# Recommender tower on one core: gathered fields first, the last tile in two parts

## The chip, the core and the metric

One core of a Trainium2 chip. The metric is the device time of one execution in microseconds. Before the change it is 455.31 us, the median of three runs (454.63 to 456.35). All times in the profile count from the start of the profiled execution's span.

## The reference

For each of 2048 samples, 50 embedding rows of 16 numbers are looked up, one per field. All 1225 dot products of two different rows go, with 16 dense numbers, through an MLP of 512, 256 and 1 units:

```python
e = jnp.stack([tbl_0[ids[:, 0]], ..., tbl_49[ids[:, 49]]], axis=1)
gram = jnp.einsum('bid,bjd->bij', e, e)[:, I_IDX, J_IDX]     # pairs i < j
...                                    # relu(cat(gram, dense) @ W_top1 + b_top1), and so on
```

29 tables have 1000 or 1250 rows ("small"), two of the 12500-row tables are called medium here, and 19 ("rest") have 12500 or 125000 rows.

## The kernel before

A tile is 128 samples; there are 16 (0 to 15; `LAST` is 15), four to a chunk; `FINAL` = 12 is the first tile of the last chunk.

**Fields.** The 19 rest fields of a tile are gathered by GpSimd, one indirect DMA per field (`gathers`, L448), through a ring of four tiles. Small and medium fields are looked up a chunk ahead as one-hot products: VectorE builds the one-hots (`compare`), TensorE multiplies (`look_up`), ScalarE copies out (`copy_lookups`), VectorE picks by the id's low bits (`pick`), and ScalarE moves the results into `split` (`move`, L1056 and L1065: 16 activations per chunk, all in the first slot of the chunk that uses them). VectorE reads a tile's gathered rows as high and low halves (`split_rows`, L576 to L589; in a chunk's first tile it waits for all moves) and turns them (`turn`, L604: `turned`, `turned2`).

**Dots.** TensorE makes all 50 x 50 dot products of a tile in small matmuls, four row groups of 32 (`dots`, L820, four groups per tile; in the last chunk `half_dots`, L841, eight halves). The results are evacuated from PSUM to `gram`: up to tile 11 by ScalarE alone (`copy_dots`, L1010), in the last chunk by ScalarE and VectorE (`copy_half`, L1018 and L644).

**Packing.** DMAs copy pieces of `gram` into `z`, 127 partitions by 11 columns, so that the first layer is 11 matmuls deep: 9 pieces for each of two sides, 18 issues on SP (`pack`, L383). For tile 15 SP, ScalarE and GpSimd issue six each. Pieces have 44, 33, 22 or 11 rows of 2816 B and five times 5 rows of 1280 B.

**MLP.** ScalarE makes the high half of z (`split_products`, L1077), VectorE the low half (L552); the first layer is 33 matmuls (`first_layer`, L881): 22 high, 11 low. Relu, transposes, layer 2 (L938), and the score on VectorE (L704, L706) follow.

**Order.** Each engine and each DMA queue runs its instructions in the order written. In slots 0 to 12, TensorE's slot T holds the dots of tile T-1, the MLP of T-3 and lookups, in eight groups; ScalarE evacuates in groups 1, 3, 5 and 7 and splits the products of T-2 in group 4. GpSimd is held only by semaphores of tile T-3 (`pace`) and T-4. The last chunk's order is written out by hand, differently on each engine. Tile 15's first nine gathered rows are read and turned together with the looked-up fields (`last_rows(0)`, L620 to L636), the last ten when they land (`last_rows(1)`); its dots wait for both:

```python
                if h == 0:
                    pe.wait_ge(turned_ready, 2 * T + (2 if T < LAST else 4))
```

Among its dots stand 16 of tile 14's 22 high matmuls (L902). Tile 15's own first layer goes in two parts by columns (L854, L858).

Of the kernel before, what the change touches and what calls it, by code (L numbers as in the profile page):

```python
# [10 lines left out]
ALU = mybir.AluOpType  # L11
# [33 lines left out]
FIELD = SMALL[:EVEN] + MED + SMALL[EVEN:] + REST  # L45
# [22 lines left out]
JS = EVEN // 2  # L68
JM = NM // 2
# [7 lines left out]
TOP = 5  # L77
PIECES = []
_p = 0
for _g in range(4):  # L80
    _r = ST * _g + TOP + 1
    PIECES.append((_r, NF - _r, ST * _g, ST, _p, 0))
    _p += NF - _r
TOP_P = _p
for _g in range(5):
    PIECES.append((ST * _g + 1, TOP, ST * _g, TOP, TOP_P + TOP * (_g // 2), TOP * (_g % 2)))
DENSE_P = TOP_P + 3 * TOP
DENSE_R = 2
# [63 lines left out]
MOVES = ((0, 1), (2, 3), (4, 5), (6, 7), (8,), (), (), ())  # L152

PIECE_INC = 16 * TWO * len(PIECES)
BIG_PIECES, CORNERS = PIECES[:6], PIECES[6:]
LAST = NTILES - 1
FINAL = (NCH - 1) * TPC
LAST_KS = (range(0, 6), range(6, ST))
LAST_J = (JS + JM, JS + JM + 5, JJ)
LAST_FIELDS = 2 * (LAST_J[1] - LAST_J[0]) - 1  # L160
HALVES = 2 * EVACS
FILL_FROM, FILL = 2, 2
# [11 lines left out]
ONE_K = ST - 1  # L174
L1_BETWEEN = 6
# [9 lines left out]
def build(nc, small, med, big, ids_small, ids_med, ids_sample, ids_big, dense, w1, w2, b2, w3, y):  # L185
    ctx = ExitStack()
    with ctx:
# [64 lines left out]
        hid_last = gram_ps[:, 0, :]  # L252
# [52 lines left out]
        corners_in = sem("corners_in")  # L305
# [32 lines left out]

        block = ctx.enter_context(nc.Block())
# [5 lines left out]
        def _(sp):  # L345
# [20 lines left out]
            def pack(T, sides=range(TWO), pieces=PIECES):  # L366
# [7 lines left out]

                if T < FINAL:
                    sp.wait_ge(gram_copied, TWO * EVACS * (T + 1))
                else:
                    sp.wait_ge(half_by_act, halves_of(T))
                    sp.wait_ge(half_by_dve, halves_of(T))
                for a in sides:  # L380
                    for piece in pieces:
                        out, src = piece_of(piece, T, a)
                        sp.dma_start(out, src).then_inc(packed[T % 2], 16)  # L383

# [38 lines left out]
            pack(NTILES - 1, (0,), BIG_PIECES)  # L423

        @block.gpsimd
        def _(pool):
# [14 lines left out]
            def gathers(T):  # L441
# [27 lines left out]
            for a in range(TWO):  # L469
                for piece in CORNERS:  # L470
                    out, src = piece_of(piece, LAST, a)
                    pool.dma_start(out, src).then_inc(corners_in, 16)

        @block.vector
        def _(dve):
# [89 lines left out]
            def rows_by_parity(T):  # L565

                t = T % TPC
                return [(emb[:, t, 1 - a:NR:2, :], split[:, t, JS + JM + 1 - a:JJ, 0, :, a],
                         split[:, t, JS + JM + 1 - a:JJ, 1, :, a]) for a in range(2)]

            def split_rows(T):
# [10 lines left out]
                known = JS + JM  # L582
                if t == 0:
# [3 lines left out]
                        split[:, :, 0:known, 2, :, :].rearrange("p t j d a -> p t j (d a)"),  # L587
                        split[:, :, 0:known, 0, :, :].rearrange("p t j d a -> p t j (d a)"))
                nc.vector.tensor_copy(  # L589
                    split[:, t, known:JJ, 2, :, :].rearrange("p j d a -> p j (d a)"),  # L590
                    split[:, t, known:JJ, 0, :, :].rearrange("p j d a -> p j (d a)")).then_inc(dve_step, 1)
# [14 lines left out]
            def last_rows(x):  # L606

                T, j0, j1 = LAST, LAST_J[x], LAST_J[x + 1]
                t = T % TPC
                if x == 0:  # L610
                    dve.wait_ge(gathered[t], 16 * NR * (T // TPC) + 16 * LAST_FIELDS)
                else:
                    dve.wait_ge(gathered_last, 16 * (NR - LAST_FIELDS))
                runs = []
                for a in range(2):
                    first = max(j0, JS + JM + 1 - a)
                    f0, f1 = (2 * (j - JS - JM) - 1 + a for j in (first, j1))
                    runs.append((emb[:, t, f0:f1 - 1:2, :], split[:, t, first:j1, 0, :, a], split[:, t, first:j1, 1, :, a]))
# [647 lines left out]
```

## Time and profile before

| | before |
|---|---|
| median of three runs | 455.31 us |
| profiled execution | 453.39 us |
| its span | 451.3 us |
| TensorE / VectorE / ScalarE / GpSimd busy | 76 / 66 / 44 / 71% |
| granted TensorE clock, mean over the span | 0.89 |

Queues and engines are named PE (TensorE), PEld (its weight loads), DVE (VectorE), ACT (ScalarE), POOL (GpSimd) and SPq (SP's DMA issues). Busy shares are averages over stages with different limits: lookups run through the first three quarters, gathers to slice 37 of 40, and only the last chunk's MLP is left then. How long a wait was, and what ended it, stands in brackets at the end of a row.

### The profile page before, as it was taken

What the parts mean: (1) busy time and instruction counts of PE and PEld (TensorE: products, weight loads), DVE (VectorE), ACT (ScalarE), POOL (GpSimd) and SP (SyncE); (2) the same over time, 40 slices, a digit from 0 to 9 for tenths busy, and PEclk for the clock granted to TensorE, in tenths of its full rate; (3) what the DMA queues carried; (4) which work ended last, traced back from release to release, by engine and by line L of the source; (5) the groups of instructions that cost most, each with busy time, mean ns of one, the idle gap of its engine ahead of it and who ended that gap; (6) DMA issues with size and microseconds to landing.
All of it is one profiled execution on the core that took longest, in us unless ns stands there. A gap on an engine that the chain in (4) does not pass through costs nothing.

```text
span 451.3 us, 13158 instructions
## 1 busy us (share of the span) xinstructions
PE 342.9 (76%) x5633; PEld 247.4 (55%) x5633; DVE 295.8 (66%) x606; ACT 198.8 (44%) x288; POOL 322.7 (71%) x318
## 2 busy tenths in 40 slices
PE   0568167566488979979989699798895948989886
PEld 0567067565366657666666476656653525454543
DVE  2599899999357579758576687566715437165551
ACT  2335712246235774455457653445487324140511
POOL 5788777777777777787777777778777777776020
PEclk9978659978679997989999969699998895988999
DMA  6994503423321344243213433111121222212020
GB/s 161 407 367 142 173 7 101 118 77 86 82 44 39 104 115 94 63 136 88 47 32 103 115 95 65 36 43 36 40 53 24 66 50 50 48 15 61 5 61 1
DMA packets 24638, 38.92 MB, mean 86 GB/s; under 512 B 8532, under 2 KB 15876, under 8 KB 24452
## 3 DMA queue, kind: packets, MB, share of 16 engines
q1 hardware_dynamic: 14166, 35.04, 24.0%
q0 software_dynamic: 9920, 2.55, 6.6%
q8 instruction: 44, 0.72, 0.7%
q10 hardware_dynamic: 494, 0.49, 0.3%
q14 instruction: 14, 0.11, 0.1%
HBM read 26.98 MB, written 0.14 MB: 60 GB/s over the span
## 4 chain that ended last, share of the span: by engine, by line
PE 34%; DVE 18%; ACT 13%; SPq 11%; issue 10%; DMA 8%; POOL 5%; another core or an unknown queue 0%; DVEq 0%; ACTq 0%; POOLq 0%
PE hid_ps L881 12%; SPq L383 11%; DVE onehot L490 9%; PE look_ps L803 8%; ACT gram L1010 6%; POOL emb L448 5%; DMA ids_bc<-ids_dram 5%; PE mid_ps L938 5%; PE gram_ps L820 3%; ACT z_both L1077 2%; DVE turned L604 2%; PE gram_ps L841 2%; ACT looked L1047 2%; DMA z_both<-gram 2%; DVE w_sb L672 1%
## 5 line engine op out<-in xcount | busy, mean ns | idle before, releaser
L448 POOL DMA_INDIRECT emb<-tbl,gidx x304 | 318.9, 1049 | 95.7 <-issue 88.4
L881 PE MATMUL hid_ps<-w_sb,z_both 127*128 127x512 f16 x462 | 112.3, 386 | 0.0
L803 PE MATMUL look_ps<-parts,onehot 125*128 125x64 f16 x1836 | 75.0, 203 | 44.5 <-DVE onehot L490 29.9
L490 DVE TENSOR_SCALAR onehot<-ids_bc,rows 125x2048 f16<-125x2048 f16 (+1 forms) x144 | 92.2, 690 | 19.2 <-PE look_ps L803 14.7
L803 PEld LDWEIGHTS look_ps<-parts,onehot 125*128 125x128 f16 x1836 | 69.5, 105 | 56.2 <-issue 20.8
L1010 ACT ACTIVATE gram<-gram_ps 50x784 f32<-50x784 f32 x96 | 78.2, 815 | 29.6 <-PE gram_ps L820 26.7
L803 PE MATMUL look_ps<-parts_med,onehot 125*128 125x128 f16 x800 | 57.1, 233 | 14.4 <-DVE onehot L490 13.8
L881 PEld LDWEIGHTS hid_ps<-w_sb,z_both 127*128 127x128 f16 x462 | 41.5, 99 | 46.1 <-issue 3.3
L803 PEld LDWEIGHTS look_ps<-parts_med,onehot 125*128 125x128 f16 x800 | 53.1, 105 | 20.6 <-DVE parts_med L663 13.9
L490 DVE TENSOR_SCALAR onehot<-ids_bc,rows_med 125x1024 f16<-125x1024 f16 x100 | 45.8, 495 | 28.2 <-PE look_ps L803 24.4
L1047 ACT ACTIVATE looked<-look_ps 128x1024 f16<-128x1024 f32 (+1 forms) x28 | 26.7, 954 | 67.0 <-PE look_ps L803 66.6
L820 PE MATMUL gram_ps<-turned 32*128 32x100 f16 x1536 | 28.6, 216 | 25.4 <-ACT gram L1010 23.1
L604 DVE STREAM_TRANSPOSE turned<-split 128x800 uint32<-128x800 uint32 x30 | 46.6, 1625 | 0.5
L938 PE MATMUL mid_ps<-w_sb,h_turned 128*128 128x256 f32 x120 | 37.8, 469 | 2.8 <-ACT h_turned L1106 2.1
L820 PEld LDWEIGHTS gram_ps<-turned 32*128 32x128 f16 x1536 | 20.8, 99 | 31.3 <-ACT gram L1010 25.9
L552 DVE SCALAR_TENSOR_TENSOR z_both<-z_both 127x704 f16<-127x704 f32 x30 | 25.3, 884 | 12.3 <-ACT z_both L1077 12.3
L1102 ACT ACTIVATE h<-hid_ps 128x512 f32<-128x512 f32 x14 | 8.4, 597 | 56.4 <-PE hid_ps L881 51.8
L938 PEld LDWEIGHTS mid_ps<-w_sb,h_turned 128*128 128x128 f32 x120 | 27.2, 238 | 8.5 <-ACT h_turned L1106 2.9
L1077 ACT ACTIVATE z_both<-z_both 127x1408 f16<-127x1408 f32 x15 | 20.6, 1371 | 11.1 <-DMA z_both<-gram 11.1
L644 DVE TENSOR_SCALAR gram<-gram_ps 50x392 f32<-50x392 f32 x32 | 17.4, 568 | 11.7 <-PE gram_ps L841 11.6
L1018 ACT ACTIVATE gram<-gram_ps 50x392 f32<-50x392 f32 x32 | 15.3, 490 | 21.4 <-PE gram_ps L841 21.2
L841 PE MATMUL gram_ps<-turned 32*128 32x100 f16 x512 | 17.4, 223 | 8.8 <-DVE turned L604 5.2
(74 smaller groups left out, 221.7 us busy)
## 6 DMA issues: line engine op xcount, KB each, us to landing
ids_bc<-ids_dram SPq DMA_DIRECT2D x28, 512.0 KB
emb<-tbl,gidx POOLq DMA_INDIRECT x304
z_both<-gram SPq DMA_DIRECT2D x31, 121.0 KB
z_both<-w SPq DMA_DIRECT2D x1, 2816.0 KB
z_both<-gram SPq DMA_DIRECT2D x31, 90.8 KB
z_both<-gram SPq DMA_DIRECT2D x152, 6.2 KB
z_both<-gram SPq DMA_DIRECT2D x31, 60.5 KB
gram<-small SPq DMA_DIRECT2D x2, 512.0 KB, 5.1
```

The lines of the kernel that those rows point to most:

```text
L383: sp.dma_start(out, src).then_inc(packed[T % 2], 16)
L448: pool.indirect_dma_start(emb[:, T % TPC, f, :], None, big[f], bass.IndirectOffsetOnAxis(ap=gidx[:, T, f:f + 1], axis=0)).then_inc(landed, 16)
L490: nc.vector.tensor_scalar(onehot[0:TP, s % RING, 0:cnt, :], ids_bc[0:TP, o % IDS_BUFS, 0:cnt, :], row, None, ALU.is_equal).then_inc(onehot ...
L604: nc.vector.transpose(out, src[:, :, w0:w0 + WORDS]).then_inc(turned_ready, 1)
L803: last = nc.tensor.matmul(bank[:, half, at:at + width], onehot[0:TP, at_ring, i, t * TILE:(t + 1) * TILE], moving.rearrange("p i s d -> p ...
L820: last = nc.tensor.matmul(gram_ps[:, r, i * TWO * NF:(i + 1) * TWO * NF], turned[p, T % 2, b:b + TWO, :].rearrange("p a m -> p (a m)"), bu ...
L841: last = nc.tensor.matmul(gram_ps[:, r, i * TWO * NF:(i + 1) * TWO * NF], turned[p, T % 2, b:b + TWO, :].rearrange("p a m -> p (a m)"), bu ...
L881: return nc.tensor.matmul(hid_ps[:, :], z_parts[0:KP, T % 2, x, k, :], w1_sb[0:KP, k, w, :], start=(i == 0), stop=(i == L1_MM - 1))
L938: last = nc.tensor.matmul(out_ps, h1_turned[:, n, :], w2_sb[:, n, :], start=(n == 0), stop=(n == N1 - 1))
L1010: nc.scalar.activation(out, src, ACT.Copy, scale=1.0 / (SCALE * SCALE)).then_inc(gram_copied, 1)
L1047: nc.scalar.activation(out, src, ACT.Copy).then_inc(looked_ready, 1)
L1077: nc.scalar.activation(halves(T, 0), products(T), ACT.Copy, scale=ZSCALE).then_inc(z_hi, 1)
```

## The change

Rest fields stand first in the order of fields, then the odd small field, the other small ones, and the medium ones. A pair (i, j) stays where row > column, so the columns of fields 0 to 9 hold every pair with one of the ten first rest fields. These ten are gathered last in every tile. For tile 15, `half_dots` computes columns 10 to 49 as soon as nine gathered rows are turned; `late_dots` computes columns 0 to 9, after all its halves and tile 14's high matmuls. The late columns are two pieces of 49 and 44 rows (1280 B each), the other seven have 39 to 21 rows of 1536 B and 15 to 5 rows of 1280 B. Of tile 15 SP and GpSimd issue the seven early pieces of a side, then SP and ScalarE the two late ones. Of tiles 13 and 14 SP issues 12 pieces and ScalarE 6. Moves of a chunk stand in the last slot of the chunk before, groups 5 to 7, but for the medium ones. The last chunk's order is rewritten on TensorE, VectorE and ScalarE. The diff, cut:

```diff
-FIELD = SMALL[:EVEN] + MED + SMALL[EVEN:] + REST
+FIELD = REST + SMALL[EVEN:] + SMALL[:EVEN] + MED
...
-JS = EVEN // 2
-JM = NM // 2
+JR = (NR + 1) // 2
+JM = JR + EVEN // 2
...
-TOP = 5
-PIECES = []
+LATE = 10
+LATE_K = 5
+PIECES = [(1, NF - 1, 0, LATE_K, 0, 0), (LATE_K + 1, NF - LATE_K - 1, LATE_K, LATE_K, NF - 1, 0)]
 _p = 0
-for _g in range(4):
...
+for _c in range(LATE, 34, ST - LATE_K):
+    PIECES.append((_c + 1, NF - _c - 1, _c, ST - LATE_K, _p, LATE_K))
+    _p += NF - _c - 1
+_p = sum(nr for _, nr, c, *_ in PIECES if c < LATE)
+for _c in range(34, NF - 1, LATE_K):
+    PIECES.append((_c + 1, NF - _c - 1, _c, LATE_K, _p, 0))
+    _p += NF - _c - 1
+LATE_PIECES, EARLY_PIECES = PIECES[:2], PIECES[2:]
+SP_PIECES, ACT_PIECES = PIECES[:3], PIECES[3:]
+DENSE_P = _p
+DENSE_R = 4
...
-MOVES = ((0, 1), (2, 3), (4, 5), (6, 7), (8,), (), (), ())
+MOVES_AHEAD = ((), (), (), (), (), (0, 1), (2, 3, 4), (5, 6, 7))
+MOVES = ((8,), (), (), (), (), (), (), ())
...
-LAST_KS = (range(0, 6), range(6, ST))
+LAST_KS = (range(LATE_K, ST), range(LATE_K))
...
-        hid_last = gram_ps[:, 0, :]
+        hid_last = look_ps[:, 1, :]
...
-                for a in sides:
-                    for piece in pieces:
+                for a in range(TWO):
+                    for piece in (PIECES if a == 0 or T <= FINAL else SP_PIECES):
...
+            def pack_last():
+                begin_pack(LAST)
+                sp.wait_ge(half_by_act, halves_of(LAST))
+                sp.wait_ge(half_by_dve, halves_of(LAST))
+                for piece in EARLY_PIECES:
...
+                sp.wait_ge(late_by_act, Q)
+                for piece in LATE_PIECES:
...
-                for f in range(NR):
-                    landed = gathered[T % TPC] if T < LAST or f < LAST_FIELDS else gathered_last
-                    pace(T, f)
+                for i in range(NR):
+                    f = (LATE + i) % NR
+                    landed = gathered[T % TPC] if T < LAST or f >= LATE else gathered_last
+                    pace(T, i)
...
+                j0, j1 = ((LATE // 2, JR), (0, LATE // 2))[x]
...
                     dve.wait_ge(half_done, halves_of(T - 2))
-                    j0 = 0
+                    j1 = JJ
+                else:
+
+                    dve.wait_ge(half_done, halves_of(T))
...
+            split_products(FINAL - 1)
+            score(FINAL - 2)
             split_rows(FINAL + 1)
             turn(FINAL + 1)
-            split_products(FINAL - 1)
+            split_products(FINAL)
             for h in range(HALVES):
                 copy_half(FINAL + 1, h)
-            score(FINAL - 2)
-            split_products(FINAL)
             score(FINAL - 1)
+            split_products(LAST - 2)
+            score(FINAL)
             split_rows(LAST - 1)
             turn(LAST - 1)
             for h in range(HALVES):
                 copy_half(LAST - 1, h)
-            split_products(LAST - 2)
+            score(LAST - 2)
             last_rows(0)
-            score(LAST - 3)
-            last_rows(1)
             for h in range(HALVES):
                 copy_half(LAST, h)
+            last_rows(1)
             split_products(LAST - 1)
-            score(LAST - 2)
+            for r in range(Q):
+                copy_late(r)
+            split_last(0)
             activate(LAST - 1)
+            split_last(1)
             copy_turned(LAST - 1, N1, mlp_copied)
-            for i in range(len(LAST_KS)):
-                split_last(i)
...
+                j0 = LATE if T == LAST else 0
...
+            def late_dots():
+
+                T = LAST
+                pe.wait_ge(turned_ready, 2 * T + 4)
+
+                pe.wait_ge(half_by_act, halves_of(T))
+                pe.wait_ge(half_by_dve, halves_of(T))
+                for h in range(2):
+                    for b in range(0, SPQ, TWO):
+                        for buf in (turned, turned2):
+                            for r in range(Q // 2 * h, Q // 2 * (h + 1)):
...
+                                    buf[p, T % 2, b:b + TWO, 0:LATE], start=(buf is turned), stop=(buf is turned2))
+                    last.then_inc(late_done, 1)
...
+            first_part(FINAL - 1, 0, L1_MM)
             for h in range(HALVES):
                 half_dots(FINAL + 1, h)
-            first_part(FINAL - 1, 0, L1_MM)
-            mlp(FINAL - 1, TURN_STEP)
-            first_part(FINAL, 0, L1_BETWEEN)
-            mlp(FINAL - 1, L2_STEP)
-            first_part(FINAL, L1_BETWEEN, L1_MM)
+                if h == TURN_AT:
+                    mlp(FINAL - 1, TURN_STEP)
+                if h == L2_AT:
+                    mlp(FINAL - 1, L2_STEP)
+            first_part(FINAL, 0, L1_MM)
+            mlp(FINAL, TURN_STEP)
+            mlp(FINAL, L2_STEP)
+            high_part(LAST - 2)
+            low_part(LAST - 2)
             for h in range(HALVES):
                 half_dots(LAST - 1, h)
-            mlp(FINAL, TURN_STEP)
-            mlp(FINAL, L2_STEP)
-            first_part(LAST - 2, 0, L1_MM)
-            mlp(LAST - 2, TURN_STEP)
-            mlp(LAST - 2, L2_STEP)
-            fill = 0
+                if h == TURN_AT:
+                    mlp(LAST - 2, TURN_STEP)
+                if h == L2_AT:
+                    mlp(LAST - 2, L2_STEP)
             for h in range(HALVES):
                 half_dots(LAST, h)
-                if h >= FILL_FROM:
-                    high_part(LAST - 1, fill, fill + FILL)
-                    fill += FILL
-            high_part(LAST - 1, fill, 2 * ST)
+            high_part(LAST - 1)
+            late_dots()
             low_part(LAST - 1)
+            last_high(0)
+            last_low(0)
             mlp(LAST - 1, TURN_STEP)
+            last_high(1)
             mlp(LAST - 1, L2_STEP)
+            last_low(1)
             last_mlp()
...
+                    if T % TPC == TPC - 1:
+                        for q in MOVES_AHEAD[g]:
+                            move(T // TPC + 1, q)
...
             split_products(FINAL - 1)
+            copy_mlp(FINAL - 1, FEED - 1)
+            split_products(FINAL)
             for h in range(HALVES):
                 copy_half(FINAL + 1, h)
-            split_products(FINAL)
-            copy_mlp(FINAL - 1, FEED - 1)
-            copy_mlp(FINAL - 1, TURN_STEP + 1)
+                if h == TURN_AT:
+                    copy_mlp(FINAL - 1, TURN_STEP + 1)
+            pack(FINAL + 1)
             copy_mlp(FINAL, FEED - 1)
-            for h in range(HALVES):
-                copy_half(LAST - 1, h)
             copy_mlp(FINAL, TURN_STEP + 1)
             split_products(LAST - 2)
             copy_mlp(LAST - 2, FEED - 1)
-            copy_mlp(LAST - 2, TURN_STEP + 1)
-            split_products(LAST - 1)
+            for h in range(HALVES):
+                copy_half(LAST - 1, h)
+                if h == TURN_AT:
+                    copy_mlp(LAST - 2, TURN_STEP + 1)
+            pack(LAST - 1)
             for h in range(HALVES):
                 copy_half(LAST, h)
-            pack(LAST, BIG_PIECES)
+            split_products(LAST - 1)
+            for r in range(Q):
+                copy_late(r)
+            pack_late()
```

## Rows read from the trace of the kernel before

**Rows 1.** The page's busy tenths in 40 slices of the span, GpSimd's line.
```profile
POOL 5788777777777777787777777778777777776020
```

**Rows 2.** Groups by line, GpSimd: count, busy us, mean ns, idle before and its releasers.
```profile
L448 POOL DMA_INDIRECT emb<-tbl,gidx x304 | 318.9, 1049 | 95.7 <-issue 88.4 <-DMA gidx<-ids_big 2.6 <-PE gram_ps L820 2.3
```

**Rows 3.** Timeline of VectorE: start us, us, engine, line, tiles, shapes [idle before].
```profile
319.83 0.40 DVE L576 TENSOR_SCALAR split<-emb 128x144 f16<-128x144 f32 x2
...
343.63 0.44 DVE L576 TENSOR_SCALAR split<-emb 128x144 f16<-128x144 f32 x2 [9.70 <-DMA emb<-tbl,gidx]
...
368.53 0.40 DVE L576 TENSOR_SCALAR split<-emb 128x144 f16<-128x144 f32 x2 [8.61 <-DMA emb<-tbl,gidx]
...
393.90 0.64 DVE L576 TENSOR_SCALAR split<-emb 128x144 f16<-128x144 f32 x2
...
409.23 2.50 DVE L636 STREAM_TRANSPOSE turned<-split 128x640 uint32<-128x640 uint32 x2
...
417.30 0.32 DVE L620 TENSOR_SCALAR split<-emb 128x80 f16<-128x80 f32 x2 [4.65 <-DMA emb<-tbl,gidx]
```

**Rows 4.** Timeline of SP's DMA queue: the packs of tiles 10 to 14.
```profile
329.29 13.41 SPq L383 DMA_DIRECT2D z_both<-gram  x18
...
349.46 13.40 SPq L383 DMA_DIRECT2D z_both<-gram  x18
...
363.44 13.43 SPq L383 DMA_DIRECT2D z_both<-gram  x18
...
380.37 14.10 SPq L383 DMA_DIRECT2D z_both<-gram  x18
...
404.46 13.44 SPq L383 DMA_DIRECT2D z_both<-gram  x18
```

**Rows 5.** Timeline of ScalarE, slots 11 and 12: evacuations, moves, split of tile 10.
```profile
327.60 1.66 ACT L1010 ACTIVATE gram<-gram_ps 50x784 f32<-50x784 f32 x2
...
335.11 2.77 ACT L1065 ACTIVATE split<-looked 128x256 f16<-128x256 f16 x8
...
343.88 1.38 ACT L1077 ACTIVATE z_both<-z_both 127x1408 f16<-127x1408 f32 x1 [1.14 <-DMA z_both<-gram]
...
347.77 1.66 ACT L1010 ACTIVATE gram<-gram_ps 50x784 f32<-50x784 f32 x2 [0.35 <-PE gram_ps L820]
```

**Rows 6.** Waits of VectorE: us in total, times, longest.
```profile
DVE split L586 <- ACT split L1056: 6.6, 2, 3.5
```

**Rows 7.** DMA issues of two lines: ns min/median/max, first and last start.
```profile
L383 SPq DMA_DIRECT2D z_both<-gram x276: 668/691/1817, 107.3 to 432.5; - x138
...
L357 SPq DMA_DIRECT2D ids_bc<-ids_dram x32: 319/320/674, 7.1 to 263.7; - x32
```

**Rows 8.** Groups by line, VectorE from 345 to 452 us.
```profile
L644 DVE TENSOR_SCALAR gram<-gram_ps 50x392 f32<-50x392 f32 x32 | 17.4, 568 | 11.7 <-PE gram_ps L841 11.6
...
L552 DVE SCALAR_TENSOR_TENSOR z_both<-z_both 127x704 f16<-127x704 f32 x10 | 8.4, 884 | 2.7 <-ACT z_both L1077 2.7
...
L704 DVE TENSOR_TENSOR h<-mid_ps,b_sb 128x256 f32<-128x256 f32 x7 | 3.0, 424 | 13.5 <-PE mid_ps L938 11.3 <-PE mid_ps L874 2.1
```

**Rows 9.** Timeline of TensorE's matmuls in the last chunk.
```profile
372.78 1.15 PE L841 MATMUL gram_ps<-turned 32*128 32x100 f16 x32 [5.21 <-DVE turned L604]
...
405.50 3.78 PE L938 MATMUL mid_ps<-w_sb,h_turned 128*128 128x256 f32 x8 [0.69 <-ACT h_turned L1106]
...
419.12 1.99 PE L938 MATMUL mid_ps<-w_sb,h_turned 128*128 128x256 f32 x8 [0.69 <-ACT h_turned L1106]
421.04 0.73 PE L841 MATMUL gram_ps<-turned 32*128 32x100 f16 x32
...
427.85 2.76 PE L902 MATMUL hid_ps<-w_sb,z_both 127*128 127x512 f16 x12
...
443.15 1.24 PE L858 MATMUL gram_ps<-w_sb,z_both 127*128 127x512 f16 x5
```

**Rows 10.** Windows: stretch, us, busy us (instructions) per engine, clock, DMA share, GB/s.
```profile
372.80:383.00 10.20, 8.44 (x137) 5.51 (x138) 8.00 (x15) 5.06 (x9) 8.07 (x8) 0.50 0.19 38
```

More of the change, by code:

```diff
@@ L364, in load_sample_ids, with begin_pack @@
                 sp.dma_start(odd[:, n % 2, :, :], ids_sample[n, :, :, :]).then_inc(sample_in[n % 2], 16)
-            def pack(T, sides=range(TWO), pieces=PIECES):
+            def begin_pack(T):
                 if T >= 2:
@@ L468, in _ @@
             pool.wait_ge(half_by_dve, halves_of(LAST))
[L469 to L472, printed above, removed]
+            for piece in EARLY_PIECES:
+                out, src = piece_of(piece, LAST, 1)
+                pool.dma_start(out, src).then_inc(early_by_pool, 16)
         @block.vector
@@ L567, in rows_by_parity @@
                 t = T % TPC
-                return [(emb[:, t, 1 - a:NR:2, :], split[:, t, JS + JM + 1 - a:JJ, 0, :, a],
-                         split[:, t, JS + JM + 1 - a:JJ, 1, :, a]) for a in range(2)]
+                return [(emb[:, t, a:NR:2, :], split[:, t, 0:JR - a, 0, :, a], split[:, t, 0:JR - a, 1, :, a])
+                        for a in range(2)]
             def split_rows(T):
@@ L845, in half_dots @@
                 last.then_inc(half_done, 1)
+            def late_dots():
[7 more added lines that the diff above has]
+                            for r in range(Q // 2 * h, Q // 2 * (h + 1)):
+                                p = slice(32 * r, 32 * r + 32)
+                                last = nc.tensor.matmul(
+                                    gram_ps[:, r, b * LATE:(b + TWO) * LATE],
+                                    turned[p, T % 2, b:b + TWO, :].rearrange("p a m -> p (a m)"),
+                                    buf[p, T % 2, b:b + TWO, 0:LATE], start=(buf is turned), stop=(buf is turned2))
+                    last.then_inc(late_done, 1)
@@ new lines, in last_high, with last_low @@
+            def last_high(i):
+                T = LAST
+                pe.wait_ge(z_hi, T + 1 + i)
+                for k in LAST_KS[i]:
+                    for w in range(2):
+                        nc.tensor.matmul(hid_last, z_parts[0:KP, T % 2, 0, k, :], w1_sb[0:KP, k, w, :],
+                                         start=(i == 0 and k == LAST_KS[0][0] and w == 0), stop=False)
+            def last_low(i):
+                T = LAST
+                pe.wait_ge(z_split, T + 1 + i)
+                for k in LAST_KS[i]:
+                    last = nc.tensor.matmul(hid_last, z_parts[0:KP, T % 2, 1, k, :], w1_sb[0:KP, k, 0, :],
+                                            start=False, stop=(i == 1 and k == LAST_KS[1][-1]))
+                if i == 1:
+                    last.then_inc(mlp_done, 1)
@@ L847, in last_mlp @@
             def last_mlp():
                 T = LAST
-                for i, ks in enumerate(LAST_KS):
-                    pe.wait_ge(z_hi, T + 1 + i)
-                    for k in ks:
-                        for w in range(2):
-                            nc.tensor.matmul(hid_last, z_parts[0:KP, T % 2, 0, k, :], w1_sb[0:KP, k, w, :],
-                                             start=(k == 0 and w == 0), stop=False)
-                    pe.wait_ge(z_split, T + 1 + i)
-                    for k in ks:
-                        last = nc.tensor.matmul(hid_last, z_parts[0:KP, T % 2, 1, k, :], w1_sb[0:KP, k, 0, :],
-                                                start=False, stop=(k == ST - 1))
@@ L1093, in pack, with pack_late @@
                 act.wait_ge(half_by_dve, halves_of(T))
-                for piece in pieces:
+                for piece in ACT_PIECES:
                     out, src = piece_of(piece, T, 1)
                     act.dma_start(out, src).then_inc(packed[T % 2], 16)
+            def pack_late():
+                act.wait_ge(z_split, LAST - 1)
+                act.wait_ge(late_by_dve, Q)
+                for piece in LATE_PIECES:
+                    out, src = piece_of(piece, LAST, 1)
+                    act.dma_start(out, src).then_inc(late_in, 16)
             def copy_mlp(T, g):
```

114 lines of the change are left out of this document (66 added, 48 removed).

## The prediction

> **What bounds the kernel now.** I read four views in this order. The page's busy slices come first: GpSimd is busy from the first slice to slice 37 of 40 and then stops [rows 1]. The groups by line show why: 304 gathers of 1.05 us with 0.3 us of issue behind each, 318.9 + 95.7 = 414.6 us, and of the 95.7 us of gaps 88.4 are that issue [rows 2]. So the gathers run back to back, and the last rows land at 417.3 us, where VectorE has waited 4.65 us for them [rows 3]. No kernel of this form ends before that; the other engines decide only the 34.0 us from there to the end of the span (451.3).
>
> The timelines of VectorE and of SP's DMA queue come next. Compute has caught up with the gathers by the last chunk: tile 11's rows are read at 319.83 with no wait for a DMA, tiles 12 and 13 are waited for (9.70 and 8.61 us), tile 14 is read at 393.90 [rows 3]. The reader is to see in SP's queue that every tile's packing is 18 issues in 13.4 us, about 0.74 each, back to back [rows 4]; ScalarE's split of tile 10 starts at 343.88, 1.2 us after the last issue (329.29 + 13.41) [rows 4, 5]. So a tile's products are ready for the MLP about 16 us after its dots are evacuated. Between pack 10 and pack 11 lie 20.17 us, and they are one chain: issue 13.41, landing 1.2, split 1.38, two pairs of evacuations with a matmul group between (345.2 to 349.4) [rows 4, 5]. Last, the TensorE timeline of the end: the last tile's dots start at 421.04, not at the landing, since layer 2 of tile 13 (419.12, 1.99 us) stands ahead of them [rows 9]; 30.3 us follow to the end.
>
> **The change, part by part.**
>
> *The new pieces.* Still 9 per side, as many bytes, but rows of 1280 or 1536 B instead of mostly 2816. Issue is 0.668 to 0.75 us over both old shapes [rows 7], so nothing suggests that the price is per row. Ends: 18 x 0.71 = 12.8 us and today's 13.4; I take 0.73, 13.1 for 18 and 8.8 for 12. The transfers lie under the issue (DMA engines are busy 0.19 there [rows 10]). If that cover went, the landing of 1.2 us would grow.
>
> *Moves ahead.* Of a chunk's 16 moves 10 now stand on ScalarE between the third and the fourth evacuation of slots 3, 7 and 11, and 5 behind the fourth. Eight cost 2.77 us [rows 5], so ten cost 3.5 us ahead of the evacuation that releases the pack. What goes: VectorE's wait for the last move, 6.6 us in two chunks, 3.3 each [rows 6]. Upstream these cancel. For tile 10, in slot 11, they don't: a tile's 19 gathers take 19 x 414.6/304 = 25.9 us [rows 2], so tile 11's rows land near 343.6 - 25.9 = 317.7, 2 us before they are read, and the first move waits until they are turned (4.6 later): with 3.5 of moves, a 0.6 copy and the 1.66 of the evacuations pack 10 can't start before some 328. Now it starts at 329.29; it moves by -1 to +3.5 us. I take +2.7, near the upper end, as the moves stand on the path plainly: 332.0. GpSimd does not feel it: it has no gap beyond issue [rows 2].
>
> *Pack 11 and 12.* Pack 11 follows 19.9 us later (20.17 less 0.3): 351.9. SP issues all 18 of both, with 0.6 us between (362.86 to 363.44 [rows 4]): pack 12 runs from 365.6 to 378.7 and lands at 379.9, now 378.1.
>
> *Last chunk's order.* Here lies the price. ScalarE and VectorE now split tile 12's products **before** they evacuate tile 13, and tile 13's **before** VectorE reads tile 14. Queued behind the first wait are tile 13's eight evacuations, behind these its pack, behind that tile 14's rows. Step by step: ScalarE's split to 381.3 (1.38 [rows 5]), VectorE's two halves of 0.884 to 383.1, its first evacuation 0.57 [rows 8]: the third half of tile 13's dots starts at 383.8. Today tile 13's dots begin at 372.78 [rows 9]. TensorE has done tile 11's first layer by then (products 369.4, 33 matmuls of 0.23 us, from 2.76/12 [rows 9]: 377.0) and stands some 5 us. Two halves 1.0; layer 2 of tile 11 1.99 or 3.78 by the clock [rows 9], I take 2.9; four halves 2.8 (pairs of 2 x 0.57 and a hand-off): 390.5. SP's 12 issues 8.8 (ScalarE's 6 beside them), landing 1.2: 400.5. Split 1.4 and 1.8, the score ahead of the rows 0.9 (0.42 twice [rows 8]): 404.6. Reading and turning tile 14 takes 4.6 (393.90 to 398.5): 409.2, and its dots start at 409.5 instead of 398.8. Tile 13's first layer, 33 x 0.23 from 401.9, ends there too. Tile 14's eight halves, 5.6, with layer 2 of tile 13 inside, 2.0: 417.0. Score 0.9, first rows of tile 15 0.9, turn 2.50 [rows 3]: the last tile's early dots start at **421.6**, today 421.04.
>
> So what the change prepares does not happen: the last rows have lain there since 417.3 when the part that was to run ahead of them begins.
>
> *The end.* What moves out of the way is tile 13's MLP, 10 us of TensorE. What comes in: pack 14 starts at 417.1 and lands at 427.1 (today at 419.1, unhurried). Split to 428.5; tile 14's 22 high matmuls 5.1: 433.6, and only then the late dots. The trace has no such matmul with 20 columns. Lower end: a fifth of the time of 100 columns, 0.6 us for 128; upper end: full price twice, 6; in the nearest row 32 take 0.73, 23 ns each [rows 9], and as each loads as many weights as before I take 3.1: 436.7. Two short evacuations 0.6, two issues 1.5, landing 1.2: 440.2; the seven early pieces on SP and GpSimd (5.1 us from 427) lie under that, as do the narrower early evacuations. The new wait of the last rows' turn for the early dots costs nothing, as the high part of tile 14 is later. TensorE's first group for tile 15 starts near 440.0 behind ScalarE's two issues: 18 x 0.23 = 4.1, transposes 0.6, 10 x 0.23, layer 2 of tile 14 2.0, 5 x 0.23: 450.2. From the last such matmul to the end of the span stay 451.3 - 444.4 = 6.9 us [rows 9]: **457.1**, against 451.3: +5.8.
>
> The profiled execution took 453.39 us, 2.1 over its span; it would be 459.2. The median shown is 455.31: **461.1**.
>
> *The clock.* After TensorE had stood 5.21 us ahead of 372.78, the granted clock was 0.50, its lower level of 1.2 GHz, for 10.2 us [rows 9, 10]. The order now leaves two such gaps, near 378 and 417. The Trainium skill says the same on its page "TensorE: Matmul & The Clock Gate" (section "Why this matters for your kernels"): avoid standing gaps between bursts, or the next burst runs at the lower level. The trace agrees by the 0.50. The rule speaks against this change; what it would cost is the second rival.
>
> **Rivals.**
>
> 1. *As designed, faster.* If a piece of at most 1536 B per row is issued at the price of the loads of ids, 0.32 us [rows 7], a pack costs 6.5 us. Pack 11 starts at 347.5 and pack 12 lands near 368, before tile 13's rows; tiles 13 and 14 are read as they land (393.3), tile 14's dots end at 406, the early dots run from 411 to 416, the late rows are turned at 419 as they land, the late dots stand behind tile 14's high part until 425, and the same end follows: 444.4, 6.9 less: **448.4**. Above about 0.5 us an issue tile 14 is late again. For it: 128-row loads do cost 0.32. Against: the five-row pieces of 1280 B, nearest to the new shape, have never been below 0.668.
> 2. *The clock too, slower.* If it is low over the whole of tile 13's layer 2 (+0.9) and, after the second gap, for ten us from 421.6, the first 3.3 us of tile 14's high part run at half speed (+1.7): **463.7**. Against it: 421.6 and after are bursts.
> 3. *No change.* The earlier chunks win as much as slot 11 loses (pack 10 at 329.1, -2.9), issue is 0.71 (-1.6) and tile 11's layer 2 finds the higher clock (-0.9): **455.7**. For it: the 6.6 us [rows 6]. Against: they are spent in slots 4 and 8, and 3, 7 and 11 pay 3.5 each.
>
> **How the numbers follow.** Forecast 0.50, rival 1 0.17, rival 2 0.13, rival 3 0.20. What a measurement can tell from no change is 0.5%, 2.3 us: below 453.0 is faster, above 457.6 slower. Hence faster 0.17, same 0.20, slower 0.63. The forecast's own range is 457.6 to 464 (pack 10 -2.9 to +0.8, late dots -2.5 to +2.9, not all at once). The range is 454.0 to 467.0: it leaves out rival 1 and a little above.
>
> **What would show it.** Right: SP's packs 11 to 14 start near 352, 365.6, 390.6 and 417; TensorE idles before the third half of tile 13's dots, released by the split of tile 12; tile 14's rows wait for the split of tile 13, not for a DMA; the last rows are read 5 us or more after landing; the late dots follow tile 14's high part. Wrong: issues under 0.5 us, or VectorE waiting for the gathers at tiles 14 and 15; then rival 1 holds. If pack 10 starts by 329.5, the moves cost nothing and rival 3 is near.

## The result and the profile after the change

The changed kernel takes 472.61 us (median of 4 runs, 470.01 to 473.42), the kernel before 454.97 beside it: a ratio of 1.0407, 95% interval 1.0362 to 1.0451 (ratios, here and below, are taken over the runs and are not the quotient of the two medians). The profiled execution took 472.1 us, its span 470.3. The forecast was 461.1 in a range of 454.0 to 467.0: slower was right, the size was not.

| us from the span's start | before | forecast | after |
|---|---|---|---|
| pack 10 begins | 329.29 | 332.0 | 340.19 |
| pack 11 | 349.46 | 351.9 | 360.84 |
| pack 12 | 363.44 | 365.6 | 375.37 |
| third half of tile 13's dots | | 383.8 | 394.29 |
| pack 13 | 380.37 | 390.6 | 401.97 |
| tile 14's rows read | 393.90 | 404.6 | 416.65 |
| pack 14 | 404.46 | 417.1 | 428.71 |
| last tile's early dots | 421.04 | 421.6 | 432.84 |
| last first-layer matmul ends | 444.4 | 450.2 | 462.9 |
| end of the span | 451.3 | 457.1 | 470.3 |

The table splits the miss at the end of the span, 13.2 us. At pack 10 the changed kernel is 10.9 us late, where 2.7 was forecast: 8.2 us of it. From pack 10 to the end it takes 130.1 us; 125.1 was forecast, and 122.0 it took before: the other 5.0.

The gathers answer to [rows 2] unchanged: as many, as long, as little idle beyond their issue.

```profile
L487 POOL DMA_INDIRECT emb<-tbl,gidx x304 | 318.1, 1046 | 95.4 <-issue 89.9 <-DMA gidx<-ids_big 2.6 <-PE look_ps L851 1.2
```

SP's DMA queue answers to [rows 4] (start us, us for all issues): 13.91 us for a pack of 18 instead of 13.41, and from pack 12 to pack 13 and from there to pack 14 lie 26.6 and 26.7 us, where 16.9 and 24.1 were before.

```profile
340.19 13.91 SPq L408 DMA_DIRECT2D z_both<-gram  x18
360.84 13.91 SPq L408 DMA_DIRECT2D z_both<-gram  x18
375.37 13.94 SPq L408 DMA_DIRECT2D z_both<-gram  x18
401.97 9.32 SPq L408 DMA_DIRECT2D z_both<-gram  x12
428.71 9.30 SPq L408 DMA_DIRECT2D z_both<-gram  x12
```

ScalarE in slot 11 answers to [rows 5]: between the third and the fourth pair of evacuations (L1089) stand ten moves (L1151) and one copy. The pairs begin 5.63 us apart, and pack 10 begins as the second ends.

```profile
332.89 1.65 ACT L1089 ACTIVATE gram<-gram_ps 50x784 f32<-50x784 f32 x2
334.56 1.44 ACT L1151 ACTIVATE split<-looked 128x256 f16<-128x256 f16 x4
336.03 0.60 ACT L1202 ACTIVATE h_turned<-mid_ps 128x512 f32<-128x512 f32 x1
336.52 2.09 ACT L1151 ACTIVATE split<-looked 128x256 f16<-128x256 f16 x6
338.52 1.65 ACT L1089 ACTIVATE gram<-gram_ps 50x784 f32<-50x784 f32 x2
```

VectorE answers to [rows 3]. Before, it read tile 13's rows (368.53) as they landed and tile 14's (393.90) within about a microsecond of it; now it reads them at 381.08 and 416.65, and no DMA releases them. Tile 14's are read behind VectorE's part of tile 13's split (L590), for which it has waited 11.42 us, and one score. They had landed near 392 (the last gather's start plus 2.3 us, the distance that the last rows show before). The last ten rows, which landed near 416, are read at 438.74.

```profile
381.08 0.40 DVE L614 TENSOR_SCALAR split<-emb 128x160 f16<-128x160 f32 x2
...
414.24 1.69 DVE L590 SCALAR_TENSOR_TENSOR z_both<-z_both 127x704 f16<-127x704 f32 x2 [11.42 <-ACT z_both L1163]
416.65 0.40 DVE L614 TENSOR_SCALAR split<-emb 128x160 f16<-128x160 f32 x2
...
438.74 0.32 DVE L657 TENSOR_SCALAR split<-emb 128x80 f16<-128x80 f32 x2
```

VectorE's waits answer to [rows 6] (us in total, times, longest; before, then after): the wait for the moves is gone from the list, and at its head stands the one for ScalarE's split. VectorE's two waits for gathers, 9.70 and 8.61 us in [rows 3], are gone too: nothing in the last chunk waits for them any more.

```profile
DVE z_both L552 <- ACT z_both L1077: 12.3, 6, 6.8
DVE z_both L590 <- ACT z_both L1163: 45.3, 11, 11.4
```

TensorE answers to [rows 9]: the wait ahead of tile 13's third half that the forecast named, the start of tile 14's dots (421.49), the last tile's early dots (432.84), which wait for the turn of their rows, tile 14's high part (L976), the late dots (L908) and the last tile's first layer.

```profile
394.29 1.33 PE L890 MATMUL gram_ps<-turned 32*128 32x100 f16 x32 [5.30 <-DVE gram L684]
...
421.49 0.72 PE L890 MATMUL gram_ps<-turned 32*128 32x100 f16 x32
...
432.84 0.97 PE L890 MATMUL gram_ps<-turned 32*128 32x80 f16 x32 [4.84 <-DVE turned L676]
...
440.95 7.61 PE L976 MATMUL hid_ps<-w_sb,z_both 127*128 127x512 f16 x22 [2.76 <-ACT z_both L1163]
448.49 1.69 PE L908 MATMUL gram_ps<-turned 32*128 32x20 f16 x128
450.12 2.55 PE L983 MATMUL hid_ps<-w_sb,z_both 127*128 127x512 f16 x11
453.45 2.76 PE L920 MATMUL look_ps<-w_sb,z_both 127*128 127x512 f16 x12 [0.78 <-ACT z_both L1175]
```

Windows of the same stretch, as in [rows 10] (the busy columns are PE, PEld, DVE, ACT and POOL; the one behind them is the granted clock): 0.50, the lower level of 1.2 GHz, through the early dots, 0.64 on average through tile 14's high part, 1.00, the level of 2.4 GHz, behind it.

```profile
432.80:440.90 8.10, 4.32 (x128) 3.66 (x128) 5.15 (x15) 4.59 (x9) 1.54 (x3) 0.50 0.21 61
440.95:448.50 7.55, 7.55 (x24) 2.73 (x24) 1.67 (x2) 0.00 (x0) 1.99 (x5) 0.64 0.16 44
448.50:463.00 14.50, 13.63 (x185) 7.70 (x184) 5.20 (x13) 2.59 (x7) 0.00 (x0) 1.00 0.06 18
```

### The profile page after: what moved, and what is told of

Same layout as the page of the kernel before. It is cut to its first block, busy times and chain, and to the rows that moved or that the text cites. A ratio compares the mean times of both kernels' runs of the same rounds, so it can differ in the third digit from the quotient of the medians.

```text
span 470.3 us, 13426 instructions
## 1 busy us (share of the span) xinstructions
PE 346.8 (74%) x5761; PEld 250.6 (53%) x5761; DVE 297.2 (63%) x610; ACT 199.5 (42%) x292; POOL 322.4 (69%) x319
## 4 chain that ended last, share of the span: by engine, by line
SPq 28%; PE 24%; ACT 15%; DVE 15%; DMA 11%; issue 6%; ACTq 0%; DVEq 0%
SPq L408 28%; PE look_ps L851 7%; DVE onehot L528 7%; ACT gram L1089 6%; DMA ids_bc<-ids_dram 5%; PE hid_ps L956 5%; DMA z_both<-gram 5%; ACT z_both L1163 3%; ACT split L1151 3%; PE hid_ps L976 3%; PE mid_ps L1012 3%; PE gram_ps L868 2%; DVE w_sb L718 1%; ACT looked L1132 1%; DVE turned L641 1%
## 5 line engine op out<-in xcount | busy, mean ns | idle before, releaser
L956 PE MATMUL hid_ps<-w_sb,z_both 127*128 127x512 f16 x429 | 104.1, 384 | 1.2 <-DVE z_both L590 1.0
L1089 ACT ACTIVATE gram<-gram_ps 50x784 f32<-50x784 f32 x96 | 78.2, 815 | 29.7 <-PE gram_ps L868 28.2
L851 PE MATMUL look_ps<-parts_med,onehot 125*128 125x128 f16 x800 | 60.0, 239 | 14.3 <-DVE onehot L528 13.8
L851 PEld LDWEIGHTS look_ps<-parts_med,onehot 125*128 125x128 f16 x800 | 55.7, 108 | 20.6 <-DVE parts_med L709 13.9
L956 PEld LDWEIGHTS hid_ps<-w_sb,z_both 127*128 127x128 f16 x429 | 37.9, 98 | 42.7 <-issue 1.8
L1132 ACT ACTIVATE looked<-look_ps 128x1024 f16<-128x1024 f32 (+1 forms) x28 | 26.7, 955 | 72.0 <-PE look_ps L851 71.9
L590 DVE SCALAR_TENSOR_TENSOR z_both<-z_both 127x704 f16<-127x704 f32 x30 | 25.4, 887 | 45.3 <-ACT z_both L1163 45.3
L868 PE MATMUL gram_ps<-turned 32*128 32x100 f16 x1536 | 27.5, 211 | 33.3 <-ACT gram L1089 31.1
L1012 PE MATMUL mid_ps<-w_sb,h_turned 128*128 128x256 f32 x120 | 39.0, 481 | 2.5 <-ACT h_turned L1202 2.5
L1012 PEld LDWEIGHTS mid_ps<-w_sb,h_turned 128*128 128x128 f32 x120 | 28.6, 251 | 8.6 <-ACT h_turned L1202 3.3
L890 PE MATMUL gram_ps<-turned 32*128 32x100 f16 (+1 forms) x512 | 16.1, 224 | 12.3 <-DVE gram L684 7.0
L684 DVE TENSOR_SCALAR gram<-gram_ps 50x392 f32<-50x392 f32 (+1 forms) x32 | 16.5, 546 | 13.4 <-PE gram_ps L890 13.1
L1097 ACT ACTIVATE gram<-gram_ps 50x392 f32<-50x392 f32 (+1 forms) x32 | 14.4, 471 | 21.9 <-PE gram_ps L890 21.7
```

Of the source, the lines that this page charges most:

```text
L590: last = nc.vector.scalar_tensor_tensor(halves(T, 1)[:, :, a, :], products(T)[:, :, a, :], ZSCALE, halves(T, 0)[:, :, a, :], ALU.mult, ALU ...
L851: last = nc.tensor.matmul(bank[:, half, at:at + width], onehot[0:TP, at_ring, i, t * TILE:(t + 1) * TILE], moving.rearrange("p i s d -> p ...
L868: last = nc.tensor.matmul(gram_ps[:, r, i * TWO * NF:(i + 1) * TWO * NF], turned[p, T % 2, b:b + TWO, :].rearrange("p a m -> p (a m)"), bu ...
L956: return nc.tensor.matmul(hid_ps[:, :], z_parts[0:KP, T % 2, x, k, :], w1_sb[0:KP, k, w, :], start=(i == 0), stop=(i == L1_MM - 1))
L1012: last = nc.tensor.matmul(out_ps, h1_turned[:, n, :], w2_sb[:, n, :], start=(n == 0), stop=(n == N1 - 1))
L1089: nc.scalar.activation(out, src, ACT.Copy, scale=1.0 / (SCALE * SCALE)).then_inc(gram_copied, 1)
```

## The experiments

The change has four parts that can be taken back: the new field order with its pieces (the layout), the moves ahead, the last tile in two parts, and the order of tiles 12 to 14. The medians are of 4 to 10 runs, with the kernel before at 454.06 (e1 to e4) and 454.03 (e5 to e8) beside them; it was 453.68 beside e9 and e10. An x is a part as in the changed kernel:

| kernel | layout | moves ahead | two parts | new order | us | ratio, 95% interval |
|---|---|---|---|---|---|---|
| e3 | x | | | | 454.09 | 0.9977 to 1.0044 |
| e6 | x | x | | | 457.07 | 1.0030 to 1.0103 |
| e5 | x | | x | | 459.67 | 1.0035 to 1.0182 |
| e2 | x | x | x | | 465.19 | 1.0194 to 1.0264 |
| e1 | x | | x | x | 468.56 | 1.0221 to 1.0338 |
| e8 | x | x | x | x | 471.52 | 1.0284 to 1.0453 |

### The moves back (e1)

```diff
-MOVES_AHEAD = ((), (), (), (), (), (0, 1), (2, 3, 4), (5, 6, 7))
-MOVES = ((8,), (), (), (), (), (), (), ())
+MOVES_AHEAD = ((),) * 8
+MOVES = ((0, 1), (2, 3), (4, 5), (6, 7), (8,), (), (), ())
```

> Changed kernel with the moves back in the chunk's first slot. Theory A (each pack starts when the fourth evacuation is done, so the ten moves ahead of it in slots 3, 7 and 11 are late packs, and the lateness stays): pack 10 starts about 4 us earlier than the changed kernel's 340.2 (334 to 337.5), the end as well: about 468.5 us (467 to 470.5). Rival B (the moves only change places and TensorE or the gathers set the pace up to tile 12): pack 10 within 1 us of 340.2, time within 1 us of 472.6.

Measured: 468.56 us, pack 10 at 336.97: both numbers are theory A's. ScalarE's third pair of evacuations in slot 11 begins where it did in the changed kernel (332.86 against 332.89), the fourth 2.42 us later instead of 5.63:

```profile
332.86 1.65 ACT L1089 ACTIVATE gram<-gram_ps 50x784 f32<-50x784 f32 x2
334.53 0.60 ACT L1202 ACTIVATE h_turned<-mid_ps 128x512 f32<-128x512 f32 x1
335.28 1.66 ACT L1089 ACTIVATE gram<-gram_ps 50x784 f32<-50x784 f32 x2 [0.16 <-PE gram_ps L868]
```

So in slot 11 the moves hold the evacuation, and pack 10 with it, back by 3.2 us, about the 3.5 of the prediction; the other 7.7 of its 10.9 us are not theirs.

### The layout alone (e3)

The kernel before with only FIELD, PIECES and the gather order changed, the rows' places following from them:

```diff
-FIELD = SMALL[:EVEN] + MED + SMALL[EVEN:] + REST
+FIELD = REST + SMALL[EVEN:] + SMALL[:EVEN] + MED
...
-                for f in range(NR):
+                for i in range(NR):
+                    f = (LATE + i) % NR
```

> Kernel before with the new order of fields, pieces and gathers alone; order, moves and tile 15's single set of dots as before. Theory A: 18 issues take 13.9 instead of 13.4 us, so pack 10 starts 3 to 6 us later than 329.3, but TensorE's 5 us of standing ahead of tile 13's dots take most of it: 455 to 459. Rival D (the shape of the pieces is free): pack 10 within 1 us of 329.3, time within 1 us of 455.0.

Measured: 454.09 us, no change: pack 10 is theory A's, the time is below A's range and within rival D's, so neither is right as a whole. SP's queue:

```profile
334.97 13.91 SPq L382 DMA_DIRECT2D z_both<-gram  x18
355.57 13.91 SPq L382 DMA_DIRECT2D z_both<-gram  x18
370.11 14.20 SPq L382 DMA_DIRECT2D z_both<-gram  x18
384.94 14.28 SPq L382 DMA_DIRECT2D z_both<-gram  x18
404.90 13.95 SPq L382 DMA_DIRECT2D z_both<-gram  x18
```

Pack 10 is 5.7 us late and pack 14 0.4: the lateness is real and is taken up. VectorE shows where (start us, us, engine, line): with the old order it still waits for tile 13's gathers and reads tile 14's rows at 394.23, against 393.90 in [rows 3].

```profile
367.37 0.40 DVE L576 TENSOR_SCALAR split<-emb 128x160 f16<-128x160 f32 x2 [1.99 <-DMA emb<-tbl,gidx]
...
394.23 0.40 DVE L576 TENSOR_SCALAR split<-emb 128x160 f16<-128x160 f32 x2
```

A second profile of the kernel before (e10) tells whether 329.29 was an early run:

> The kernel before once more, for a second profile of it: pack 10 at 329.3 within 1.5 us if the 5.7 us by which it came later under the new layout are the layout's; near 333 to 335 if the first profile of the kernel before was an early one upstream. Time 452 to 456.

```profile
328.47 13.40 SPq L383 DMA_DIRECT2D z_both<-gram  x18
```

It was not (454.05 us): the lateness belongs to the layout. In e1 above and e5, e7 and e9 below the work up to there is the same as in e3, and pack 10 begins at 336.08 to 337.31 in them: the 5.7 us of e3 are the least of five profiles.

Where it comes from is argued, not shown. Ten packs of 13.91 instead of 13.40 us would make 5.1 us if every slot passed its own on. Not every slot does: ScalarE's split stands still for a pack in 5 of 15 tiles before and in 7 of 15 in e3 (us in total, times, longest), and in the other tiles it does not wait for one.

```profile
ACT z_both L1077 <- DMA z_both<-gram: 11.1, 5, 8.9
ACT z_both L1077 <- DMA z_both<-gram: 21.5, 7, 9.7
```

From 107 to 329 us the means of the engines' recurring work are the same in both traces (an evacuation 0.815 us, a split 1.372), and the granted clock is 0.90 in e3 against 0.91 and, in e10, 0.93. That makes the issue the likely cause and the clock a small rival; no run changes either alone.

### The order of tiles 12 to 14 back (e2)

```diff
-            split_products(FINAL - 1)
-            score(FINAL - 2)
             split_rows(FINAL + 1)
             turn(FINAL + 1)
-            split_products(FINAL)
+            split_products(FINAL - 1)
```

and so on, as in the kernel before, on VectorE, ScalarE and TensorE, with all 18 issues of each pack on SP.

> Changed kernel with the order of tiles 12 to 14 and their packing (18 issues on SP) as before the change; tile 15 stays in two parts. Theory A: the splits that stand ahead of tile 13's evacuations and tile 14's rows are the larger part of the loss: tile 14's rows are read by 400 instead of 416.7, the time falls by 10 us or more, to 457 to 462. Rival C (the loss is in packs 0 to 10, 11 us late, and the order only passes it on): the time falls by less than 4 us, 469 or more.

Measured: 465.19 us: between the two theories, so "10 or more" was missed. Packs 13 and 14 begin at 390.97 and 410.35, 11 and 18 us earlier than in the changed kernel (after the same pack 10, 340.49), yet the end comes only 6.7 earlier: tile 13's MLP stands behind tile 14's dots again, and from pack 14 to the last tile's early dots it takes 17.1 us instead of 4.1.

### The late dots ahead of tile 14's high part (e4)

```diff
-            high_part(LAST - 1)
             late_dots()
+            high_part(LAST - 1)
```

> Changed kernel with the late dots ahead of tile 14's high matmuls on TensorE. Theory A (at the end TensorE is the bound, so the two only change places): within 1.5 us of 472.6. Rival E (what is late there is the last pieces' way through two DMA queues): late pieces land 7 us earlier and the time falls by 4 us or more, to 468.5 or less.

Measured: 467.55 us (ratio 1.0257 to 1.0346). The time is in rival E's range, but not for E's reason alone: everything up to pack 10 is the changed kernel's, and yet pack 10 began at 335.85; profiles of the same code differ by some 4 us there. From pack 14 on it took 39.9 us against 41.6, so the edit is worth 1.7 us, a little more than theory A allows and less than the 4 of E. To see the spread, the changed kernel once more (e8):

> The changed kernel itself, to see how far two runs of it differ upstream: pack 10 between 335.5 and 341 and the time between 467 and 473, the two moving together, if the 4 us by which pack 10 differed between the changed kernel and the one with the late dots first belong to the run and not to the edit.

471.52 us, pack 10 at 338.77, and 41.7 us from pack 14 to the end of the span. Both numbers lie in their ranges; that the two move together is what e4 and e8 suggest, not more.

### The last tile in two parts, alone (e5), and the moves alone (e6)

e5 is e2 with the moves back too; e6 is e3 with the moves ahead. In e2 and e5 one thing besides the two parts differs from the kernel before: VectorE makes tile 13's score ahead of the last tile's evacuations.

> The changed kernel with the moves and the order of tiles 12 to 14 both as before: only the new field order with its pieces and the last tile in two parts stay. Theory P (the price of the last tile in two parts is its own: its early dots are no longer woven into tile 14's first layer, and tile 14's split waits behind their evacuation): 459 to 463, some 6 to 8 us above the kernel before, pack 14 within 1 us of 405 and the first-layer matmuls of tile 14 starting 4 or more us later than in the kernel before (422.86, its first two). Rival Q (the two parts cost nothing by themselves; the +11 with the old order was the moves ahead, +4, and a late pack 14): 453 to 456.

> The kernel before with the new field order and pieces and the moves of the next chunk taken ahead; order of the last chunk and last tile as before. Theory M (the moves ahead push every pack from slot 7 on back by some 4 us, more than the old order has room for after the 5.7 us that the layout took): pack 10 near 339, 457 to 460. Rival N (the old order still takes it up before the last tile's dots at 421): pack 10 near 339 as well, but 453 to 456. If pack 10 is near 335, the moves cost nothing without the new order.

e5: 459.67 us, theory P. TensorE of e5:

```profile
419.86 1.99 PE L1012 MATMUL mid_ps<-w_sb,h_turned 128*128 128x256 f32 x8 [0.69 <-ACT h_turned L1198]
421.79 0.63 PE L890 MATMUL gram_ps<-turned 32*128 32x80 f16 x32
...
428.87 6.31 PE L976 MATMUL hid_ps<-w_sb,z_both 127*128 127x512 f16 x22 [1.78 <-ACT z_both L1159]
435.11 1.69 PE L908 MATMUL gram_ps<-turned 32*128 32x20 f16 x128
436.73 2.55 PE L983 MATMUL hid_ps<-w_sb,z_both 127*128 127x512 f16 x11
440.75 2.76 PE L920 MATMUL look_ps<-w_sb,z_both 127*128 127x512 f16 x12 [1.47 <-ACT z_both L1171]
```

Pack 14 is on time (405.12) and the early dots begin where the whole last tile began before (421.04 [rows 9]): nothing was won by having the early part ready, as TensorE is busy with layer 2 of tile 13 (419.86) until then. Behind them comes more than before: the high part waits 1.78 and then runs at a granted clock of 0.77, the late dots take 1.69, the first layer waits 1.47. From the early dots to the end of the span lie 36.0 us, where 30.3 were before.

e6: 457.07 us, theory M, at the low edge of its range (runs from 455.0 to 462.0). Pack 10 is at 339.11 and pack 14 at 410.52: of 9.8 us at pack 10, 6.1 are left at pack 14, where e3's 5.7 had shrunk to 0.4.

### The weave back (e9), and the early dots moved forward (e7)

e9 is e5 with the early dots between pairs of tile 14's high matmuls, as the kernel before has them:

```diff
             for h in range(HALVES):
                 half_dots(LAST, h)
-            high_part(LAST - 1)
+                if h >= 2:
+                    high_part(LAST - 1, fill, fill + 2)
+                    fill += 2
+            high_part(LAST - 1, fill, 2 * ST)
```

with tile 14's split ahead of the evacuation of tile 15 on ScalarE, and tile 13's score on VectorE where the kernel before has it.

> As e5_two_parts_only, but the early dots of tile 15 stand in eighths between pairs of tile 14's first-layer matmuls, as the kernel before has them, and tile 14's split comes ahead of the evacuation of tile 15. Theory P (the +5.6 of the two parts is the lost weave: TensorE waits for evacuations and for tile 14's split, and then runs tile 14's high part at the lower clock): 454.5 to 457, no wait ahead of tile 14's first-layer matmuls, those at about 0.22 to 0.25 us each. Rival L (the +5.6 is the second part itself: late dots, late evacuation and late pieces behind the early ones): 458.5 to 461, with TensorE waiting ahead of the last tile's first layer for as long as the weave has saved.

Measured: 458.53 us (12 runs, 454.35 to 461.28; ratio 1.0042 to 1.0122): rival L by its time, at the lower edge, and by its wait; theory P's sign came true as well, as tile 14's matmuls run without a wait at 0.23 us each. TensorE of e9, and its clock behind the wait:

```profile
429.08 2.76 PE L977 MATMUL hid_ps<-w_sb,z_both 127*128 127x512 f16 x12
431.77 1.79 PE L908 MATMUL gram_ps<-turned 32*128 32x20 f16 x128
433.50 2.55 PE L984 MATMUL hid_ps<-w_sb,z_both 127*128 127x512 f16 x11
438.19 4.08 PE L920 MATMUL look_ps<-w_sb,z_both 127*128 127x512 f16 x12 [2.14 <-ACT z_both L1176]
442.06 1.87 PE L928 MATMUL look_ps<-w_sb,z_both 127*128 127x512 f16 x6
...
438.20:443.70 5.50, 5.50 (x18) 2.24 (x19) 2.49 (x5) 0.74 (x1) 0.00 (x0) 0.69 0.00 2
```

The weave runs at the full clock, but TensorE then waits 2.14 us for ScalarE's split of the early part and, at a granted clock of 0.69, runs 18 matmuls in 5.95 us that took 4.21 before (2.76 and 1.46 in e5). From the early dots (422.80) to the end of the span lie 33.9 us: of the 5.7 us that e5 lost there the weave gives back 2.1, and 3.6 stay. They are about the second part's own: 1.8 us of late dots, 2.1 of wait and 1.7 of clock, less the two waits ahead of tile 14's transposes and layer 2 that the kernel before has there (0.88 and 0.79). Another 1.7 us of e9's lateness was there at pack 14 (406.20).

e7 is e5 with the early dots further ahead, the orders on VectorE and ScalarE following:

```diff
-            first_part(LAST - 2, 0, L1_MM)
+            for h in range(HALVES):
+                first_part(LAST - 2, 4 * h, 4 * h + 4)
+                half_dots(LAST, h)
+            first_part(LAST - 2, 4 * HALVES, L1_MM)
...
-            for h in range(HALVES):
-                half_dots(LAST, h)
-            high_part(LAST - 1)
             late_dots()
+            high_part(LAST - 1)
```

> As e5_two_parts_only, but the early dots of tile 15 are woven into tile 13's first layer (four matmuls, an eighth of the dots, and so on), tile 14's split comes ahead of tile 13's evacuation, and the late dots stand ahead of tile 14's high part. Theory P: the last tile's dots leave the place behind layer 2 of tile 13; TensorE is the bound from 409 on and only its gaps there (some 4 us up to 437) can be saved: 449 to 453, early dots beginning near 411, late dots near 422. Rival R (the late rows, their transposes, evacuation and pieces are a chain of their own of some 36 us from the landing near 416, as in the changed kernel from pack 14's neighbourhood): 454 to 458, with TensorE idle more than 3 us ahead of the last tile's second part.

Measured: 459.30 us (ratio 1.0024 to 1.0177), above both theories. The early dots began at 414.44 and the late ones at 431.52, not 422: tile 13's first layer now ends at 424.8 instead of the 417.8 of e5, and behind it stands the same queue. From the early dots on TensorE waits nowhere more than 2.03 us: it is all but full there, and what is moved ahead of tile 13 pushes tile 13 back.

No kernel here beats the kernel before; the layout alone equals it.

## Why the prediction failed, point by point

**What bounds the kernel.** Right for the gathers. Right too that the last tile's dots stand behind tile 13's MLP and not behind the landing; e5 and e7 bear out that this leaves the two parts nothing to win.

**The new pieces: the step that failed.** The prediction took 0.73 us an issue, "13.1 for 18", between 12.8 and today's 13.4, from single issues of 0.668 to 0.75. It measured 13.91, 0.773 each: above the upper end. From start to start [rows 4] already give 0.745 (13.41/18), so 0.73 made the new pieces cheaper than the old. And the price went into packs 11 and 12 only: for pack 10 the sum has the moves and nothing for the layout, without a reason ("Upstream these cancel" is said of the moves). The layout alone put pack 10 at 334.97 (e3), where 332.0 stood for everything, and at up to 337.31 in the other four runs that have it without the moves. How much of that the longer issue makes is not shown.

**Moves ahead.** 3.5 us ahead of the evacuation: 3.2 measured in slot 11. That they cancel upstream was right: between the five profiles with the moves ahead and the five without, packs 2, 6 and 10, right behind moves, come 3.1, 2.2 and 2.4 us later on average, but packs 3, 7 and 9 0.6 to 0.9 earlier. VectorE's wait for them did go. In the whole the moves ahead cost 3.0 us (e8 less e1, e6 less e3; 5.5 from e5 to e2).

**Last chunk's order.** Mechanism as forecast, place by place: the third half of tile 13's dots waits for the split of tile 12, tile 14's rows for the split of tile 13. Pack 11 to pack 14 took 67.9 us, forecast 65.2. What the forecast did not see is what it does to lateness. With the old order, tiles 13 and 14 are read when they land, and 5.7 us at pack 10 are 0.4 at pack 14 (e3). With the new one tile 14's rows wait for two splits behind two packs, 24 us past their landing, and what is late at pack 10 stays late. From pack 10 to pack 14 the four runs with the new order (e1, e4, e8 and the changed kernel) take 88.5 to 89.5 us, whether pack 10 begins at 335.85 or at 340.19. With the old order it is 75.2 and 75.5 us in the kernel before, and 69.0 to 71.4 in the six runs with the new layout: it takes up some 5 us and no more. That is why the step above weighs so much here: 8.2 of the 13.2 us missed are there at pack 10. The order's own price is 8.9 us (e1 less e5), or 6.3 where the moves have used up the room already (e8 less e2).

**The end.** The late dots took 1.69 us, not 3.1. Tile 14's high part took 7.61, not 5.1, since the early dots before it ran with gaps of 4.84 and 2.76 us around them: granted clock 0.50 and then 0.64. That is rival 2's mechanism, with 22 matmuls at 4.92 elsewhere in the same trace (414.26): +2.7 us against its +1.7. Its other half came too: layer 2 amid tile 13's dots took 3.50 us, where 2.9 stood in the forecast. The Trainium skill's page "TensorE: Matmul & The Clock Gate" (section "Why this matters for your kernels") warns of such gaps, and the trace agrees by the 0.50 behind the 4.84; the prediction gave it a chance of 0.13 where its own forecast had the second gap.

**The rivals.** Rival 1 needed an issue of 0.32 us: it is 0.773. Rival 3 needed the earlier chunks to win: pack 6 is 10.7 us late (248.12 against 237.45), and in none of the ten profiles with the new layout are packs 6 to 10 earlier than before. Neither holds.

**The sum.** In the working, 417.1 with 0.9, 0.9 and 2.5 is 421.4 and not 421.6, and if rival 1's late dots end at 425, the same end (13.5 and 6.9 us behind them) gives 445.4 and not 444.4; neither matters here. One path from the kernel before to the changed one: layout +0.0 (454.06 to 454.09), two parts +5.6 (to 459.67, e5), order +8.9 (to 468.56, e1), moves +3.0 (to 471.52, e8). Medians of four runs that spread by up to 5 us carry each term to some 2 us, and the terms depend on the order in which they are taken. That the layout costs nothing at the end holds with the old order; the new order without the new layout was not run, so how much of its 8.9 us is the layout's lateness coming through is not split.

**Open:** why an issue of the new pieces takes 0.773 us, how much of the lateness at pack 10 that makes, and why pack 10 differs by up to 4.6 us between profiles of the same upstream code (335.85 to 340.49).

## What to carry to other kernels

A price that every tile pays can come back in every tile's chain, so sum it from the first tile, not from the stage under study. Before work is split so that part of it can start earlier, look at what the engine does at that moment: if it has no idle time there, the split only adds its second part. And an order that reads new input as it lands takes up lateness from upstream; one that queues the reading behind a long chain passes it on.

## What the runs showed of the hardware that was not expected

- 128 matmuls of 32 rows by 20 columns, rotating over two of the four row groups at a time, took 1.69 us, 13 ns each; 32 of 100 columns, over two row groups as well, took 0.73, 23 ns each [rows 9], both at a granted clock of 1.00. Five times the columns cost 1.7 times as much: neither a fixed price nor one by the column.
- An issue on SP of a piece with 1280 or 1536 B per row took 0.773 us in a pack of 18 and 9.32/12 = 0.777 in a pack of 12, from start to start; the old pieces, mostly with longer rows, took 0.744. On ScalarE two such issues took 2.22 us in e5 and 1.54 in the changed kernel.
- 22 matmuls of 512 columns took 4.92 us at 414.26 and 7.61 at 440.95 in one trace, at granted clocks of 1.00 and 0.64.
